# An SSM stage with y kept transposed, the inner norm applied behind the output projection, and output products on halves and quarters of the TensorE array

## What is computed

```python
x_t, z_t, b_t, c_t, a_log = split(x @ W_in.T)         # 32 heads, P = N = 64, inner width 2048
decay = exp(-exp(a_log))
# per token: states = states * dec + x outer b;  y = states . c + x * D
y = y * silu(z_t)
y = (y - y.mean(-1)) * rsqrt(y.var(-1) + EPS) * gamma + beta      # over the 2048 inner columns
return y @ W_out.T
```

## Time and profile before

| | us |
|---|---|
| median of three runs | 1880.67 |
| lowest, highest | 1878.51, 1883.77 |
| the profiled execution, its own time | 1884.98 |
| its span, first to last instruction | 1883.2 |
| mean granted TensorE clock, share of full | 0.972 |

### The profile page before, as it was taken

One profiled execution on the slowest core, in us unless ns is written; L12 is line 12 of the kernel. 1 busy time (PEld: TensorE's weight loads), 2 busy tenths in 40 slices (PEclk: granted clock), 3 DMA queues, 4 the chain that ended last, 5 costly groups with the idle time before them and its releaser, 6 DMA issues.

```text
span 1883.2 us, 31983 instructions
## 1 busy us (share of the span) xinstructions
PE 1742.3 (93%) x11128; PEld 1506.7 (80%) x11128; DVE 1091.5 (58%) x2215; ACT 854.1 (45%) x2288; POOL 679.6 (36%) x846
## 2 busy tenths in 40 slices
PE   5997999898999999998969969998989999999989
PEld 3885777787888889887848857777878988888878
DVE  4334888554566666666443348885445666666664
ACT  3433445323444444445533334553244444444465
POOL 1453434100255555551014533440003555555510
PEclk9997999999999999999989989999999999999989
DMA  2332010002322222330023400000032232333200
GB/s 73 99 125 86 18 35 1 1 1 83 87 95 93 93 93 93 93 97 6 14 72 108 157 33 18 34 1 1 1 107 65 98 96 100 96 101 98 70 7 17
DMA packets 54349, 120.86 MB, mean 64 GB/s; under 512 B 6560, under 2 KB 15264, under 8 KB 53680
## 3 DMA queue, kind: packets, MB, share of 16 engines
q1 hardware_dynamic: 54192, 118.83, 19.4%
HBM read 116.12 MB, written 2.69 MB: 63 GB/s over the span
## 4 chain that ended last, share of the span: by engine, by line
PE 54%; issue 15%; DVE 14%; POOL 10%; ACT 5%; DMA 2%; SPq 1%; POOLq 0%; DVEq 0%; ACTq 0%
PE ps L497 20%; PE ps L554 12%; PE ps L789 4%; PE ps L546 3%; POOL silu_g L411 3%; PE ps L533 2%; PE ps L770 2%; POOL y L474 2%; PE ps L794 2%; POOL rb L429 2%; DVE yg L1494 2%; POOL fw_lo L396 2%; PE ps L664 2%; PE ps L665 2%; PE ps L645 2%
## 5 line engine op out<-in xcount | busy, mean ns | idle before, releaser
L474 POOL TENSOR_TENSOR y<-yg,sz 128x128 f32<-128x128 f32 x256 | 211.6, 827 | 254.5 <-DVE yg L1494 254.5
L554 PE MATMUL ps<-w_out,yT 128*128 128x256 f32 x1024 | 226.0, 379 | 0.0
L554 PEld LDWEIGHTS ps<-w_out,yT 128*128 128x128 f32 x1024 | 192.4, 190 | 24.9
L429 POOL TENSOR_TENSOR rb<-ra,rb 128x512 f32<-128x512 f32 x80 | 118.2, 1477 | 202.8 <-DVE rb L1331 202.8
L789 PE MATMUL ps<-xz_x,mt 128*128 128x128 f32 x1024 | 170.3, 284 | 15.2 <-DVE yg L1494 10.9
L1482 DVE SCALAR_TENSOR_TENSOR ssm_state<-ssm_state,pdec,ps 64x64 f32<-64x64 f32 x448 | 124.3, 277 | 101.0 <-PE ps L780 93.5
L1494 DVE TENSOR_TENSOR yg<-ps,xd 128x128 f32<-128x128 f32 x256 | 74.7, 292 | 159.5 <-issue 92.6
L789 PEld LDWEIGHTS ps<-xz_x,mt 128*128 128x128 f32 x1024 | 139.1, 191 | 26.4 <-issue 15.9
L1454 DVE TENSOR_TENSOR_SCAN lmat<-dec,ident 128x512 f32<-128x512 f32 x128 | 155.5, 1215 | 0.0
L497 PE MATMUL ps<-w_in_hi,xnT_hi 128*128 128x256 f32 x512 | 155.1, 303 | 0.0
L1196 DVE TENSOR_TENSOR hid<-ps,silu_g 128x512 f32<-128x512 f32 (+1 forms) x80 | 55.2, 690 | 171.7 <-POOL silu_g L411 105.6
(11 more groups left out here) (162 smaller groups left out, 4543.2 us busy)
## 6 DMA issues: line engine op xcount, KB each, us to landing
dec<-dec_dram SPq DMA_DIRECT2D x64, 512.0 KB, 4.9
w_raw<-in_w_in SPq DMA_DIRECT2D x32, 512.0 KB, 4.4
pdec<-dec_dram SPq DMA_DIRECT2D x128, 128.0 KB, 2.9
fw_raw<-in_fw SPq DMA_DIRECT2D x40, 384.0 KB, 3.3
w_raw<-in_w_qkv SPq DMA_DIRECT2D x8, 768.0 KB, 4.2
comb<-comb_dram SPq DMA_DIRECT2D x8, 512.0 KB, 3.7
w_out<-in_w_o SPq DMA_DIRECT2D x2, 2048.0 KB, 10.5
w_out<-in_w_out SPq DMA_DIRECT2D x2, 2048.0 KB, 8.2
```

The lines of the kernel that those rows point to most:

```text
L429: nc.gpsimd.tensor_tensor(rb[:, k], ra[:, k], rb[:, k], ALU.add).then_inc(a_rot.sem, 1)
L474: nc.gpsimd.tensor_tensor(y[:, c, bass.ds((2 * i + w) * P, P)], yg[:, s], sz[:, s], ALU.mult).then_inc(s_out.sem, 1)
L554: mm = nc.tensor.matmul(ps[:, 4 + s, 0:DM], yT[:, s, t, :], w_out[:, t, :], start=(t == 0), stop=(t == NT - 1))
```

## The change

- **x and z** are projected like b and c, inner columns as rows, 512 tokens wide. x is copied (`x_copy`), turned by PE (`x_turn`) and copied again to token rows (`xtok_copy`); DVE weights it once per unit (`x_weighted`).
- **y stays transposed** (`yt`, inner columns as rows, 1024 tokens per pair). Each head has its own product: x of one head (128 x 64, stationary) with the decayed scores, then the state of one head (64 x 64, stationary) with `cTp`, both into that head's 64 partitions of PSUM.
- **Skip, gate and sums** are done once per unit, 512 wide: DVE adds `x * D`, POOL multiplies by silu(z), ACT squares, and POOL adds up y and its square over the head pairs (`y_sum`). POOL splits the weights two pairs ahead in one instruction of 1024. `dec`, `lmat`, `bT` and `cT` hold one unit only.
- **Phase 6** (`out_proj1`) makes no transposes: per tile of 128 inner columns ACT and DVE split `w_out` (first half only) and y times gamma into high and low parts, and PE makes 4 chunks x 3 fp32r products, 256 wide, into one PSUM bank per chunk. The mean and variance come from 16 products of `y_sum` with a column of ones, once. The norm is applied behind: `gate * rs` on ACT, `(-mean * rs * (gamma @ W_out) + beta @ W_out) * gate` added to `x_res` by ACT and POOL.
- **Once, in phase 0 of batch 0**: SP loads `w_out` for layer 1 behind the first two ffn tiles, PE makes the two rows gamma @ W_out and beta @ W_out ahead of the fifth turn, ACT copies them, SP sends them through DRAM to all partitions.

The diff, cut to what sets order and size (POOL, PE, ACT and DVE in that order behind SP's part; 12 columns of indent taken off):

```diff
+        if b == 0 and k == 1:
+            sp.dma_start(w_out[:], a["w_out"]).then_inc(w_out_in, 16)
+        if b == 0 and k == SHARED_TILES:
+            sp.wait_ge(affine_copy, 1)
+            sp.dma_start(affine_dram, affine_rows[:]).then_inc(affine_out, 16)
+            sp.wait_ge(affine_out, 16)
+            sp.dma_start(affine[:], affine_dram.partition_broadcast(P)).then_inc(affine_in, 16)
...
-            sp.wait_ge(s_scan.sem, s_scan.done(2 * (u - 2) + 1))
-            sp.dma_start(dec[:, :, toks], dec_dram[0, 2 * h:2 * h + 2, toks].partition_broadcast(P)).then_inc(dec_in[hf], 16)
+            sp.wait_ge(s_scan.sem, s_scan.done(2 * u - 1))
+            sp.dma_start(dec[:], dec_dram[0, 2 * h:2 * h + 2, toks].partition_broadcast(P)).then_inc(dec_in, 16)
...
+        pool.wait_ge(s_yg.sem, s_yg.done(u))
+        pool.wait_ge(s_z.sem, s_z.done(u))
+        nc.gpsimd.tensor_tensor(yt[:, h, toks], yg[:], sz[:], ALU.mult).then_inc(s_out.sem, 1)
+        if hf == 1 and h + 2 < HP:
+            split_lo(split_ssm(b, h + 2), w_in[h % 2][1][:], raw, w_in[h % 2][0][:])
...
+            nc.gpsimd.tensor_tensor(y_sum[0][:, toks], y_sum[0][:, toks], yt[:, h, toks], ALU.add)
+            pool.wait_ge(s_sq.sem, s_sq.done(u))
+            nc.gpsimd.tensor_tensor(y_sum[1][:, toks], y_sum[1][:, toks], y_sq[:], ALU.add).then_inc(s_acc.sem, 1)
...
+            pe.wait_ge(p_yh.sem, p_yh.done(n))
+            pe.wait_ge(p_yl.sem, p_yl.done(n))
+            for j in range(4):
+                for x, (l, r) in enumerate(SPLITS):
+                    mm = nc.tensor.matmul(ps[:, 4 * hf + j, 0:DM], ys[l][:, n % 4, j * P:(j + 1) * P], wo[r][:, t, :],
+                                          start=(t == 0 and x == 0), stop=(t == NT - 1 and x == 2))
+            mm.then_inc(p_mm.sem, 1)
+            if hf == 0 and t == 1:
+                for x in range(2):
+                    for c in range(NC):
+                        mm = nc.tensor.matmul(ps[:, 7, x * NC + c:x * NC + c + 1], y_sum[x][:, c * P:(c + 1) * P], causal[:, P - 1:P],
+                                              start=True, stop=True)
+                mm.then_inc(p_stat.sem, 1)
...
+        if b == 0 and c == NC // 2:
+            pe.wait_ge(w_out_in, 16)
+            for t in range(NT):
+                mm = nc.tensor.matmul(ps[0:2, 0, 0:DM], gamma_beta[:, t, :], w_out[:, t, :], start=(t == 0), stop=(t == NT - 1))
+            mm.then_inc(affine_mm, 1)
...
+    def x_turn(u):
+        pe.wait_ge(s_x.sem, s_x.done(u))
+        turn(2, xT[:, u % 2, :]).then_inc(s_trx.sem, 1)
...
     def ssm_outputs(u, m, c):
-        out = ps[:, 6, 0:P]
-        pe.wait_ge(s_xcopy.sem, s_xcopy.done(m))
-        pe.wait_ge(s_yg.sem, s_yg.done(m - 1))
+        toks = slice(c % 4 * P, (c % 4 + 1) * P)
+        if c % 4 == 0:
+            pe.wait_ge(s_xtok.sem, s_xtok.done(u))
+            pe.wait_ge(s_mt.sem, s_mt.done(2 * u + 1))
+            pe.wait_ge(s_yg.sem, s_yg.done(u - 1))
         for h in range(2):
-            if c % 4 == 0:
-                pe.wait_ge(s_mt.sem, s_mt.done(2 * u + h))
-            nc.tensor.matmul(out, mt1[:, u % 2, h, c % 4 * P:(c % 4 + 1) * P], xz_x[:, c % 2, h * P:(h + 1) * P],
-                             start=(h == 0), stop=False)
+            q = slice(64 * h, 64 * h + 64)
+            nc.tensor.matmul(ps[q, 6, toks], x_tok[:, c, q], mt1[:, u % 2, h, toks], start=True, stop=False, skip_group_check=True)
         if c % 4 == 0:
             pe.wait_ge(s_cp.sem, s_cp.done(u))
         pe.wait_ge(s_st.sem, s_st.done(m - 1))
-        nc.tensor.matmul(out, cTp[:, c * P:(c + 1) * P], ssm_state[:, c % 2, :], start=False, stop=True).then_inc(s_y.sem, 1)
+        for h in range(2):
+            q = slice(64 * h, 64 * h + 64)
+            mm = nc.tensor.matmul(ps[q, 6, toks], ssm_state[q, c % 2, q], cTp[q, c * P:(c + 1) * P], start=False, stop=True,
+                                  skip_group_check=True)
+        mm.then_inc(s_y.sem, 1)
 
     def ssm_unit(u):
 
-        hf = u % 2
-        n, ahead = u // 2 - b * HP, u < 2 * HP * (b + 1) - 1
-        nw, nhf = (n + hf) % 2, 1 - hf
+        ahead = u < 2 * HP * (b + 1) - 1
         for j in range(4):
-            c, m = 4 * hf + j, 4 * u + j
-            if ahead and j == 3:
-                b_turn(u + 1, nhf)
-            if ahead or j < 3:
-                project_xz(m + 1, nw if j == 3 else n % 2, (c + 1) % NC)
+            c, m = 4 * (u % 2) + j, 4 * u + j
+            if ahead and j == 0:
+                project_x(u + 1)
+            if ahead and j == 1:
+                project_c(u + 1)
+                x_turn(u + 1)
+            if ahead and j == 2:
+                project_b(u + 1)
+            if j == 3:
+                project_z(u)
...
+                if ahead:
+                    b_turn(u + 1)
...
+    def w_hi_of(t):
+        nc.scalar.activation(wo[0][:, t, :], w_out[:, t, :], ACT.Copy).then_inc(p_wh.sem, 1)
+
+    def y_hi(hf, t):
+        n = (2 * b + hf) * NT + t
+        act.wait_ge(p_mm.sem, p_mm.done(n - 4))
+        nc.scalar.activation(ys[0][:, n % 4, :], yt[:, t, hf * HALF:(hf + 1) * HALF], ACT.Copy,
+                             scale=gamma_beta[:, t, 0:1]).then_inc(p_yh.sem, 1)
...
+    def mean_shift(c):
+        n = b * NC + c
+        act.wait_ge(p_nm.sem, p_nm.done(b))
+        act.wait_ge(p_base.sem, p_base.done(3 * (n - 2) + 2))
+        nc.scalar.activation(shift[:, c % 2, :], affine[:, 0, :], ACT.Copy, scale=in_nm[:, c:c + 1]).then_inc(p_shift.sem, 1)
+
+    def gate_scaled(c):
+        n = b * NC + c
+        act.wait_ge(p_base.sem, p_base.done(3 * n + 1))
+        nc.scalar.activation(gate[:, c, :], gate[:, c, :], ACT.Copy, scale=in_rs[:, c:c + 1]).then_inc(p_gate.sem, 1)
...
+    for hf in range(2):
+        for t in range(NT):
+            if hf == 0:
+                w_hi_of(t)
+            y_hi(hf, t)
+            if hf == 0 and t == 4:
+                inner_std()
+            if t >= 7 and t % 2 == 1 and t < 15:
+                mean_shift(4 * hf + (t - 7) // 2)
+            if t >= 9 and t % 2 == 1:
+                gate_scaled(4 * hf + (t - 9) // 2)
...
+        ahead = u < 2 * HP * (b + 1) - 1
+        if ahead:
+            x_copy(u + 1)
+            c_copy(u + 1)
+            xtok_copy(u + 1)
+        if u > 2 * b * HP:
+            y_square(u - 1)
+        if hf == 0 and 1 <= h and h + 1 < HP:
+            ssm_prep(h + 1, (h + 1) % 2)
+        if ahead:
+            b_copy(u + 1)
+        z_silu(u)
+        if ahead:
+            btok_copy(u + 1)
+    u0 = 2 * b * HP
+    x_copy(u0)
+    c_copy(u0)
+    xtok_copy(u0)
+    b_copy(u0)
+    btok_copy(u0)
+    ssm_prep(1, 1)
...
+    def add_gated(c):
+        n = b * NC + c
+        dve.wait_ge(p_mm.sem, p_mm.done((2 * b + c // 4) * NT + NT - 1))
+        dve.wait_ge(p_gate.sem, p_gate.done(n))
+        dve.wait_ge(p_res.sem, p_res.done(n - 2))
+        nc.vector.tensor_tensor(sg1[:, c % 2], ps[:, c, 0:DM], chunk(gate, c), ALU.mult).then_inc(p_sg.sem, 1)
+        dve.wait_ge(p_sg.sem, p_sg.done(n))
+        dve.wait_ge(p_base.sem, p_base.done(3 * n + 2))
+        nc.vector.tensor_tensor(chunk(x_res, c), sg1[:, c % 2], chunk(x_res, c), ALU.add).then_inc(p_res.sem, 1)
...
+    for hf in range(2):
+        for t in range(NT):
+            if hf == 0:
+                w_low(t)
+            y_low(hf, t)
+            if hf == 0 and t == 3:
+                inner_variance()
+            if hf == 0 and t == 5:
+                inner_root()
+            if hf == 1 and t in (3, 6, 9, 12):
+                add_gated((t - 3) // 3)
+    for c in range(4, NC):
+        add_gated(c)
...
+    def x_weighted(u):
+
+        chunks = slice(4 * (u % 2), 4 * (u % 2) + 4)
+        ends = lmat[:].rearrange("p h (c t) -> p c h t", t=P)[:, :, :, P - 1:P].broadcast_to([P, 4, 2, 64])
+        dve.wait_ge(s_xtok.sem, s_xtok.done(u))
+        dve.wait_ge(s_scan.sem, s_scan.done(2 * u + 1))
+        dve.wait_ge(s_y.sem, s_y.done(4 * u - 5))
+        nc.vector.tensor_tensor(xw[:, chunks, :].rearrange("p c (h e) -> p c h e", h=2),
+                                x_tok[:, chunks, :].rearrange("p c (h e) -> p c h e", h=2), ends, ALU.mult).then_inc(s_xw.sem, 1)
...
-    def add_skip(m, c):
-        s = c % 2
-        dve.wait_ge(s_y.sem, s_y.done(m))
-        dve.wait_ge(s_xd.sem, s_xd.done(m))
-        dve.wait_ge(s_out.sem, s_out.free(m, 2))
-        nc.vector.tensor_tensor(yg[:, s], ps[:, 6, 0:P], xd[:, s], ALU.add).then_inc(s_yg.sem, 1)
+    def add_skip(u):
+        h = u // 2 - b * HP
+        dve.wait_ge(s_y.sem, s_y.done(4 * u + 3))
+        dve.wait_ge(s_x.sem, s_x.done(u))
+        dve.wait_ge(s_out.sem, s_out.done(u - 1))
+        nc.vector.scalar_tensor_tensor(yg[:], xT[:, u % 2, :], d_skip[:, h:h + 1], ps[:, 6, :], ALU.mult, ALU.add).then_inc(s_yg.sem, 1)
...
+            if ahead and j == 0:
+                decay_scan(u + 1, 0)
+            if ahead and j == 1:
+                decay_scan(u + 1, 1)
+                x_weighted(u + 1)
```

(50 more changed lines are left out.)

482 lines of the change are left out of this document (233 added, 249 removed).

## The result

The change made the kernel slower: 1905.57 us (median, 1904.75 to 1907.10) against 1879.59 for the kernel before on the same chip, a ratio of 1.0134 with a 95% interval of 1.012 to 1.0148. The profiled execution took 1906.31 us, its span 1904.5; against the span of before (1883.2) that is +21.3. The difference of the medians is +26.0; the profiled execution of before took 1884.98, 5.4 above its median, that of after 0.7 above its own, so about 5 us of the slowdown are missing from every comparison of the two profiles. 1926.7 was forecast, with a range of 1850 to 1985: the direction and the range hold, but 46 us were forecast and 26 came.

A forecast was written before the change was run, and what follows sets the result against it. PE, busy 93%, was taken as the bound; span 1883.2 + 64 (SSM) + 4 (stage starts) - 32 (projections) + 10 (affine row) = 1929 us, or 1926.7 against the median 1880.7 (+46); range 1850 to 1985.

The forecast's parts named there:

- The price of a switch: SSM output products and scores: each array-shape change costs PE 0.15 us to a 64-column mode, 0.20 to the full array.
- Rival 1: SSM stage: switches between these modes cost nothing (1814 us) or half (about 1870 us); chance 0.18.
- The column pair: SSM output products: a chunk's two products on column halves run side by side, 0.22 us a pair.
- Rival 2: SSM output products: the two column-half products run in series, +0.22 x 4 us a unit, +57, 1984 us; chance 0.10.
- rival 3: SSM scores: PE waits 1.5 us once a head for ACT's late copy of b, +45, 1972 us; chance 0.12.
- The unit after: One SSM unit of the changed kernel: 12.27 us, PE's 11.97 plus 0.3 of waits.
- PE's sum: One SSM unit after the change: PE's products and switches add up to 11.97 us, without waits.
- The end "none": SSM unit after the change: lower end of the assumed 0.3 us of waits, giving +45 us over 64 units.
- The unit before: One SSM unit of the old kernel: 11.27 us from stage divided by 32, 10.73 of PE and 0.54 of waits.
- Rival 4: SSM waits dearer than counted (-19) and projection shorter, no clock loss (-6), no waits left: about 1902 us; chance 0.10.
- Affine row: First phase of batch 0: PE waits for w_out, then 16 f32 products delay the fifth layer-norm turn, +10 us.
- stage start: Start of each SSM stage: ACT's preparation and gate silu delay the second unit's copies, +2 us a batch, +4.

The follow-up runs named there:

- e11: Changed kernel with each unit's eight score products split by three passes of the z projection, adding two array-shape switches in 62 units: 1930.22 us (1.0258).
- e1: Changed kernel with the state product as one full-array product per chunk instead of two on quarters: 1881.47 us (ratio 1.0006).
- e8: Changed kernel with full-array state product, a unit's column products grouped behind the third chunk's state product, x weighting read from PSUM: 1808.10 us (0.9615).
- e3: Changed kernel with a unit's column products grouped ahead of its state products, and the state product on the whole array: 1871.06 us (0.9952).
- e12: Changed kernel with 52 unused products keeping PE busy between each SSM stage and the projection behind it: 1894.29 us (1.0075).
- e2: Changed kernel with a unit's eight column products issued together ahead of its first state product, state products still on quarters: 1906.72 us (1.0141).
- e6: e2 with the accumulation opened only once per bank and DVE's weighting of x reading PSUM instead of the SBUF copy: 1887.29 us (1.0031).
- e10: Changed kernel with one edit, DVE's weighting of x reading PSUM instead of the SBUF copy: 1903.43 us (1.0121).
- e5: Changed kernel with the 16 affine products moved from the first phase to the end of batch 0's SSM stage: 1896.42 us (1.0076).
- e9: Changed kernel with the edits of e8 and e5 together: 1798.76 us (0.9565).

## Why the prediction came out as it did

- **The price of a switch** held: 0.93 us for a chunk's output block against 0.94, and 0.15, 0.15 and 0.20 for its three switches. It rested on two thin groups of rows, and e11 and e1 now stand behind it. Rival 1 (free or half) falls with them: free would have been 1814.
- **The column pair** runs side by side: eight products of e8 in 1.02 us, where 16 passes in series would be 1.8. Rival 2 falls; and the Trainium skill's rule on row groups that was set beside it ("TensorE: Matmul & The Clock Gate", Part 3) doesn't decide the products here.
- **ACT late for the scores** (rival 3): between 560 and 820 us the changed kernel has no row of it, PE waits for nothing but the shape. The mechanism was real, though: e3 took the cover away and it came out, 12.3 us in 260.
- **The unit after** was 12.03, not 12.27: PE's sum of 11.97 was right to 0.06, and of the 0.3 of waits that I put on top no row shows any. The end "none" was the right one. That is 15 us.
- **The unit before** was 11.45, not 11.27: I divided the whole stage by 32 units, and the last one, with nothing of a next unit in it, is shorter than the others. So the waits that the change removed were 0.72 us (11.45 less PE's 10.73), not 0.54, and 11 us more went away. These two are the mis-sized term, the waits of the SSM stage: +0.58 a unit measured against +1.0 (37 us over 64 units, of which the first and last units of each stage take 2 back). That the range held is owed to PE's sum, which was right in each part that the rows show, and not to errors that cancel: both errors in the waits went the same way.
- **Rival 4** is what happened in its first half: dearer waits, none left; its 1902 is the figure that came nearest to 1905.6. Its second half (no clock loss in the projection) is not: -29.1 against the -32 forecast. From the first to the last product 45.7 + 3.4 + 1 + 2 = 52.1 us were worked out and 55.4 came; the granted clock has the larger part of that. It was 0.52 in the first 5.07 us (2.2 us over the 2.88 of e12), and it fell again behind the statistics (0.50 between 911 and 915 us, as the table by stretch has it):

```profile
911.00:915.00 4.00, 4.00 (x20) 4.00 (x21) 3.79 (x14) 2.56 (x6) 0.00 (x0) 0.50 0.00 0
915.00:919.00 4.00, 4.00 (x28) 4.00 (x28) 2.60 (x5) 2.35 (x5) 1.36 (x2) 0.75 0.01 2
```

  20 products in 4 us where 33 fit at full clock: 2 us a batch were put in for the clock, some 4.5 were due (2.2, and 1.6 and 0.7 in these two rows). The start (6.8 for 8.0 us) and the tail (3.3 for 3.6) were a little better than forecast.
- **Affine row and stage start**: +10.4 for +10, +3.8 for +4. The products in the first phase ran from 19.61 to 28.17 (8.56 us for the 9.3 forecast), behind a load that was forecast to land at 20.3 and had landed by 19.61:

```profile
19.61 8.56 PE L628 MATMUL ps<-w_out,gamma_beta 128*2 128x256 f32 x32 [2.35 <-DMA w_out<-in_w_out]
```

## What to carry to other kernels

Halving the work of small products buys nothing when the changes of array shape around them cost more than it saves (0.49 us against 0.22 in a chunk here). Count switches as instructions (0.15 to 0.2 us each here), and order the work so that products of one shape stand together; the same column products that lost time in four places gained it in one. Take the period of a loop from its steady part, start to start over many rounds, and not from the stage divided by its rounds: the waits in it are what is left over, and an error there goes one to one into the forecast. When the bound has been shortened, look again at everything that was free under it: a slow neighbour (DVE at 2.86 us) cost nothing in the changed kernel and 19 us once the columns were grouped (e2 against e6), and ACT's copy, covered before, cost 12.3 us in a stretch of 260 (e3).

## What the runs showed of the hardware

- DVE's product of two SBUF operands, 128x512 f32, took 0.68 us at best, 2.03 in the mean of 64 and 2.90 at most in the changed kernel: 0.68 or 0.69 at the five places where POOL did nothing meanwhile, 2.87 to 2.90 at the 28 where POOL worked all the time. With one operand from PSUM it took 0.69 in the mean of 64, and 0.69 at most (e6, e8, e10). The Trainium skill ("VectorE: DVE Perf Modes", Two Vector instructions with no wait between them) names the second input of an operation with two SBUF inputs as read through an interface shared with GpSimd; e2 against e6 agrees, 2.86 against 0.69 us. Part of the slowness moves to its neighbour: over the same stretch the scan's mean was 1253 ns in the changed kernel and 1479 in e10, where the weighting no longer stands beside POOL in its place.
- A switch of array shape costs twice: the first pass comes 0.09 to 0.10 us late, and the second is late too, since the load ahead of it wasn't started early: 0.11 with a load of 128 columns, 0.05 with one of 64. That is 0.2 us for a switch between the full array and 64 rows (e11), and 0.15, 0.15 and 0.20 in the chain full, columns, quarters, full. The Trainium skill ("TensorEngine Tiling (Array Packing)", Key Properties) says that changing the tiling mode drains the engine; the rows agree, and the size is theirs.
- Products of one column cost 0.11 us a pass at full clock, 0.22 for a plain f32 product, as much as products 128 wide: in e12's 3.50 us of statistics the weight loads are busy for 3.50, so the load sets the beat.
- Between the affine products of e5 and the projection PE stood idle for 2.5 us only, and the clock still fell, eight products into the projection (0.62 in the mean of its first 4.39 us); in e9, with the same edit, it stayed at 1.00 for the first 2.94 us. What tells the two apart, I can't say.
